# Two edge passes of a graph network: five PSUM banks, a fifteen-pair ring, and VectorE's steps at four distances

## The reference

```
q, k, v = linear maps of x, in 8 heads of 32                    # layer one
score   = clip(sum(q[dst] * k[src]) / sqrt(32), -10, 10)        # per edge and head
alpha   = exp(score - max) / sum over the edges of dst
wv      = segment_sum(alpha * v[src], dst)
x       = feat + (wv @ Wp.T + bp)
h       = layernorm(x) * ln_g + ln_b
out     = x + (gelu(h @ W1.T + b1) @ W2.T + b2)
x       = layernorm(x_in + out)

z       = leaky_relu(x @ W_s.T [src] + x @ W_t.T [dst])         # layer two
e       = z @ W_attn.T                                          # one number per edge
alpha   = exp(e - max) / sum over the edges of src
agg     = segment_sum(alpha * x[src], dst)
out     = layernorm(x + (agg @ W_fc.T + b_fc))
```

## Time and profile before

| | |
|---|---|
| median of three runs | 4053.36 us |
| the profiled execution, its own time | 4052.72 us |
| its span, first to last instruction | 4050.9 us |
| mean granted TensorE clock | 0.766 of 2.4 GHz |
| busy: PE / DVE / ACT / POOL | 2350.9 / 2223.8 / 1218.1 / 1941.0 us |
| HBM, mean | 172 GB/s |

### The profile page before, as it was taken

The page is one execution under the profiler, slowest core; times in us unless marked ns, Lnnn a source line. Parts: engine busy times, 40 slices in busy tenths (PEclk is TensorE's granted clock), DMA queues, the critical chain, the costliest instruction groups (busy, mean ns, idle before and its releaser), DMA issues. The chain is left out here.

```text
span 4050.9 us, 56408 instructions
## 1 busy us (share of the span) xinstructions
PE 2350.9 (58%) x11454; PEld 1705.1 (42%) x11455; DVE 2223.8 (55%) x6089; ACT 1218.1 (30%) x3239; POOL 1941.0 (48%) x1970
## 2 busy tenths in 40 slices
PE   4666666666666665887333333333333396777776
PEld 2344444444444444675122222222222195566555
DVE  5565565555555563334344444444444596677675
ACT  0255555555555553333122222222222200111111
POOL 0255555555555552212655656655555303444443
PEclk9888888888888887898565666666666656888998
DMA  4666665665666662113667677666766605666664
GB/s 140 196 175 176 176 177 174 180 181 169 177 178 179 176 182 84 65 63 100 207 205 205 206 210 209 200 202 203 205 200 200 181 0 164 200 205 198 193 208 148
DMA packets 365706, 698.61 MB, mean 172 GB/s; under 512 B 77317, under 2 KB 247039, under 8 KB 365674
## 3 DMA queue, kind: packets, MB, share of 16 engines
q0 software_dynamic: 134784, 425.63, 36.1%
q1 hardware_dynamic: 220602, 256.40, 20.2%
q10 hardware_dynamic: 10288, 16.23, 1.1%
HBM read 597.23 MB, written 100.85 MB: 172 GB/s over the span
## 5 line engine op out<-in xcount | busy, mean ns | idle before, releaser
L878 PE MATMUL ps_px<-sb_parts,sb_bits 128*128 x4860 | 886.7, 344 | 902.9 <-DVEq L1590 362.3
L759 POOL DMA_INDIRECT sb_ring<-kv_rows,sb_idx x810 | 792.3, 978 | 723.8 <-DVE sb_msg L1458 377.5
L878 PEld LDWEIGHTS ps_px<-sb_parts,sb_bits 128*128 128x128 bf16 x4860 | 566.5, 121 | 1238.4 <-DVEq L1590 586.7
L888 PE MATMUL ps_pa<-sb_msg,sb_onehot 128*128 128x264 f32 x1620 | 567.5, 483 | 433.1 <-DVE sb_msg L1458 349.0
L1125 ACT ACTIVATE sb_bits<-sb_bits 128x256 bf16<-128x256 bf16 x810 | 322.7, 409 | 1019.2 <-remote 725.9
L1443 DVE TENSOR_TENSOR sb_prod<-ps_px,sb_ring 128x512 f32<-128x512 f32 x405 | 278.7, 688 | 573.7 <-remote 339.9
L888 PEld LDWEIGHTS ps_pa<-sb_msg,sb_onehot 128*128 128x128 f32 x1620 | 345.0, 235 | 551.3 <-DVE sb_msg L1458 373.6
L759 POOL DMA_INDIRECT sb_ring<-proj_rows,sb_idx x324 | 311.7, 962 | 321.8 <-issue 156.1
L759 POOL DMA_INDIRECT sb_w<-narrow_rows,sb_idx x324 | 310.1, 957 | 207.4 <-DVEq L1590 113.0
L759 POOL DMA_INDIRECT sb_w<-feat_rows,sb_idx x162 | 158.6, 979 | 426.1 <-issue 190.3
L1593 DVE SCALAR_TENSOR_TENSOR sb_prod<-sb_msg,sb_attn_hi 128x256 f32<-128x256 f32 x810 | 300.5, 421 | 0.7 <-issue 0.7
(11 more groups left out here) (242 smaller groups left out, 3070.2 us busy)
## 6 DMA issues: line engine op xcount, KB each, us to landing
sb_bits<-dst_short SPq DMA_DIRECT2D x280, 192.0 KB
x_edges<-sb_ring SPq DMA_DIRECT2D x54, 768.0 KB
sb_slots<-x_edges SPq DMA_DIRECT2D x54, 768.0 KB
x_edges<-sb_slots SPq DMA_DIRECT2D x27, 768.0 KB
sb_w<-x_edges SPq DMA_DIRECT2D x27, 768.0 KB
sb_msg<-lo_rows SPq DMA_DIRECT2D x28, 576.0 KB
sb_ring<-kv_rows,sb_idx POOLq DMA_INDIRECT x810
kv_rows<-sb_slots ACTq DMA_DIRECT2D x25, 256.0 KB, 2.8
```

What stands on the lines that cost most here:

```text
L759: pool.indirect_dma_start(out=out[:, i, :], out_offset=None, in_=rows, in_offset=bass.IndirectOffsetOnAxis(ap=idx[:, 2 * p + i:2 * p + i + ...
L878: mm = pe.matmul(px[:, j, 0:width], onehot_t[:, j, :], flat(visit_parts[:, bass.ds(parity, 1), a, 0:width]), start=(a == 0), stop=(a == 2))
L888: mm = pe.matmul(pa[:, 0:C + H], onehot[:, j, :], msg[:, j, :], start=(p == 0 and i == 0), stop=True, skip_group_check=True)
```

## The change

In pass one:
- The ring of gathered keys and values grows from 5 to 15 pairs of slots, `kv_pairs`: six in `ring`, three in `slots`, six behind the node parts in `parts`. Each pair of a visit has its own slot and its own semaphore; the semaphores are shared with pass two.
- `px` holds a pair in one bank (two halves of 256 columns). Five banks serve five pairs (FLIGHT = 5), and the sixth takes the sums of the pairs from 8 on (EARLY), so that VectorE can copy `pa` at pair 10. Expansion is issued AHEAD = 9 pairs ahead of the sum.
- VectorE's order within pair p becomes: clip of p + 3, product of p + 6, scores of p + 4, message of p. The steps at a visit's end are spread over pairs 1 to 5 of the next visit.
- Messages go to `wide`, a ring of five pairs; scores have five places. Edge one-hots keep three.
- The node one-hots are made six tiles at a time, in place, in a room for all 30 tiles of a visit (`hots_t`), four groups ahead.
- SyncE stores a visit's projected rows two visits behind, at the end of its round, and the load of x (`load_inputs(0)`) goes behind the pass.

In pass two the node one-hots work the same way, `zbuf` has five pairs, the slot is freed by the row step itself, and the three small steps come once a visit over 30 tiles; two columns of each tile are kept for them by a copy (`low_dots`), one a pair.

The diff, cut to its core:

```diff
+FLIGHT = 5
+AHEAD = 9
...
-        kv_slots = ring_flat[:, 0:S * 2 * C].rearrange("p (j c) -> p j c", j=S)
+        kv_rooms = [ring_flat[:, 0:6 * 4 * C], slots[:, 0:3 * 4 * C], parts_f[:, kv_at:kv_at + 6 * 4 * C]]
+        kv_pairs = [room[:, i * 4 * C:(i + 1) * 4 * C].rearrange("p (j c) -> p j c", j=2) for room, n in zip(kv_rooms, (6, 3, 6)) for i in range(n)]
...
-                        gather_pair(0, p, kv_slots[:, two(p), :], kv_rows, gathered[0][p % SLOTS])
+                        gather_pair(0, p, kv_pairs[p], kv_rows, gathered[p])
...
-                pe.wait_ge(hot_t[L], v * PAIRS + p + 2)
+                if p % RING == 0:
+                    pe.wait_ge(hot_t[L], v * HALVES + p // RING + 2)
...
-                for j in flight(p):
+                for i in (0, 1):
+                    into = px[:, p % FLIGHT, i * C:i * C + width] if L == 0 else px[:, 2 * (p % RING) + i, 0:width]
                     for a in range(3):
-                        mm = pe.matmul(px[:, j, 0:width], onehot_t[:, j, :], flat(visit_parts[:, bass.ds(parity, 1), a, 0:width]),
+                        mm = pe.matmul(into, hots_t[L][:, 2 * p + i, :], flat(visit_parts[:, bass.ds(parity, 1), a, 0:width]),
                                        start=(a == 0), stop=(a == 2))
...
+                if p == EARLY and earlier is not None:
+                    pe.wait_ge(nd, earlier * ND + NDS["acc"])
+                into = pa if p < EARLY else px[:, FLIGHT]
...
+            def node_onehots(L, v, h):
+
+                act.wait_ge(far[L], v * HALVES + h + 2)
+                act.activation(hots_t[L][:, half(h), :], hots_t[L][:, half(h), :], ACT.Relu, bias=1.0, scale=-1.0).then_inc(hot_t[L], 1)
...
-                if p + 2 < end:
-                    products(*ahead[1])
-                if p + 1 < end:
-                    clipped(*ahead[0])
-                messages(v, p)
-                if p + 2 < end:
-                    scores(*ahead[1])
...
+                for p in range(PAIRS):
+                    if earlier is not None and 1 <= p <= len(FINISH):
+                        finish(earlier, FINISH[p - 1])
+                    if p + 3 < PAIRS or not last:
+                        clipped(*later(v, p + 3))
+                    if p + 6 < PAIRS or not last:
+                        products(*later(v, p + 6))
+                    if p + 4 < PAIRS or not last:
+                        scores(*later(v, p + 4))
+                    messages(v, p)
+                    if p == EARLY + 2:
+                        sums_kept(v)
...
-                        dve.wait_ge(zs, base + RING + R)
-
-                        dve.tensor_tensor(dots[:, 1], dots[:, 0], zbuf[:, :, C], ALU.add).then_inc(zs, 1)
...
+                        dve.wait_ge(slots_free[1], v * PAIRS + p + 1 + PAIRS)
+                        dve.tensor_copy(low_dots[:, :, 2 * p:2 * p + 2].rearrange("p c j -> p j c"), zbuf[:, pair(p), C:CW])
...
+                    dve.tensor_tensor(dots[:, 1], dots[:, 0], low_dots[:, 0], ALU.add).then_inc(zs, 1)
...
-            load_inputs(0)
             sp.wait_ge(y_clear, 16)
             first_pass()
+            load_inputs(0)
```

More of the change, by code:

```diff
@@ L270, in build @@
         q_ready = sem("q_ready")
-        gathered = [[sem(f"gathered{L}_{p}") for p in range(n)] for L, n in enumerate((SLOTS, PAIRS))]
+        gathered = [sem(f"gathered{p}") for p in range(PAIRS)]
         gathered_x = {p: sem(f"gathered_x{p}") for p in range(PAIRS) if not streamed(p)}
@@ L394, in places, with landed, pair, half @@
             return slice(2 * (p % RING), 2 * (p % RING) + 2)
-        def two(p):
-            return slice(2 * (p % SLOTS), 2 * (p % SLOTS) + 2)
+        def landed(eng, L, total, v, p):
+            eng.wait_ge(gathered[p], (v + total) * 32 + 32 if L else v * 32 + 32)
+        def pair(p):
+            return slice(2 * (p % FLIGHT), 2 * (p % FLIGHT) + 2)
+        def half(h):
+            return slice(h * R, (h + 1) * R)
+        def later(v, p):
+            return (v, p) if p < PAIRS else (v + 1, p - PAIRS)
         def chunk(p):
@@ L568, in visit @@
                             node_parts(node, parity)
-                        if L == 0 and h == 3 and earlier is not None:
-                            products_out(earlier)
                     fetched(v, range(PAIRS - SLOTS, PAIRS))
                     indices(after, THIRDS - 1)
+                    if L == 0 and earlier is not None:
+                        products_out(earlier)
                 def first_parts():
@@ L935, in _ @@
             parity, = value()
-            for p in range(4):
+            for p in range(AHEAD):
                 expand(0, C, parity, 0, p)
@@ L1142, in exps @@
                 act.wait_ge(summed, v * PAIRS + p + 1)
[L1143 removed]
+                act.activation(sums_in[:, pair(p), C:C + H], score[:, p % FLIGHT], ACT.Exp, scale=SCORE_SCALE).then_inc(exp1, 1)
             def window_nodes(v, earlier=None):
                 if earlier is not None:
[L1149 removed]
+                    act.wait_ge(far_e, (earlier + 1) * PAIRS)
                     act.sem_inc(act_seen, 1)
@@ L1181, in visits @@
-                    if p + 1 < PAIRS:
-                        edge_onehots(v, p + 1)
-                    if earlier is not None and p == 2:
+                            node_distances(0, at, h)
+                        if p % RING == 1:
+                            node_onehots(0, at, h)
+                    if p + 1 < PAIRS:
+                        edge_distances(t0, v, p + 1)
+                    elif not last:
+                        window_nodes(v + 1, v)
+                        edge_distances(t0, v + 1, 0)
@@ L1184, in visits @@
+                    if p:
+                        edge_onehots(v, p - 1)
+                    elif earlier is not None:
+                        edge_onehots(earlier, PAIRS - 1)
+                    if earlier is not None and p == 10:
                         sums_copied(earlier)
-                    if earlier is not None and p == 6:
+                    if earlier is not None and p == PAIRS - 1:
                         product_copied(earlier)
-                    if not last and p == PAIRS - 3:
-                        node_distances(0, v + 1, 0)
-                        node_onehots(0, v + 1, 0)
@@ new lines, in _, with visits @@
+            FINISH = ["acc", "den0", "den1", "den2", "agg"]
+            def visits(v, earlier=None, last=False):
+                for p in range(PAIRS):
[10 more added lines that the diff above has]
+                        sums_kept(v)
@@ L1507, in _ @@
+            for p in range(6):
+                if p >= 3:
+                    clipped(0, p - 3)
+                products(0, p)
+                if p >= 2:
+                    scores(0, p - 2)
+            visits(0)
+            with dve.Fori(0, total - 2) as u:
+                visits(dve.snap(u + 1), u)
+            visits(last_visit(dve), visit_before(dve), last=True)
+            for step in FINISH:
+                finish(last_visit(dve), step)
             dve.sem_inc(nv, 1)
@@ new lines, in _ @@
+                    rows(0)
+                    for p in range(PAIRS):
+                        if p + 1 < PAIRS:
+                            rows(p + 1)
+                        attend(p)
+                    dve.wait_ge(zs, v * len(ZS) + ZS["dots"])
+                    dve.tensor_tensor(dots[:, 1], dots[:, 0], low_dots[:, 0], ALU.add).then_inc(zs, 1)
+                    dve.wait_ge(zs, v * len(ZS) + ZS["low"])
+                    dve.tensor_tensor(dots[:, 2], dots[:, 1], low_dots[:, 1], ALU.mult).then_inc(zs, 1)
@@ L1616, in _ @@
+                    dve.wait_ge(zs, v * len(ZS) + ZS["masked"])
+                    some = e_all[:, bass.ds(t0, G)]
+                    dve.tensor_tensor(some, some, dots[:, 2], ALU.add).then_inc(zs, 1)
+                    dve.wait_ge(zs, v * len(ZS) + ZS["added"])
+                    dve.sem_inc(dve_seen, 1)
             for c in range(THIRDS):
```

253 lines of the change are left out of this document (111 added, 142 removed).

## The result

The changed kernel takes 4004.69 us (median of four runs, 3987.71 to 4020.03) against 4052.74 for the kernel before in the same runs: a ratio of 0.988, 95% interval 0.985 to 0.991, 48 us less. Forecast was 3925. Both later comparisons gave the same ratio (0.989 and 0.988). The profiled execution took 3997.64 us, its span is 3995.8.

The account below looks back on a forecast made before the run. It took gather runs over some 7 us, which nearly stop the other engines, as the limit. From 4052.7: -100 (ring), -35 (pass two), +6 (edges) = 3924, stated as 3925 us; range 3700 to 4110.

Parts of the forecast that it names:

- What bounds the kernel: Both edge passes: made of waits, no engine full; long gather runs nearly stop the other engines and limit this change.
- over some 7 us: Both edge passes: gather runs longer than this nearly stop other engines until 1 to 2.5 us after the run ends.
- The ring, -100 us: Pass one: 15 pairs of slots instead of five take it from 3.46 to 3.21 us a pair, -100 us.
- the stop of "3 us": Pass one, POOL: pause assumed after each 10.5 us gather run, making a cycle of 13.5 us for 4.2 pairs.
- Rival C: Pass one doesn't move, run and stop lengths change but not their sum; 4024, or up to 4053; chance 0.18.
- D: Pass one slower: POOL fills 15 slots in one run, starves the others, then waits for them; 4113; chance 0.18.
- Banks and distances: Pass one: five PSUM banks and VectorE's four distances remove 153.2 us of expansion waits; counted within the ring's sum.
- Visit's end: Pass one: steps spread over the next visit, one add more (12 us of VectorE), stalls go; left inside 2.15 us a pair.
- ScalarE's one-hots: Node one-hots for three pairs at a time, three activations become one; ScalarE has slack, so worth nothing and costing nothing.
- Pass two, -35: Pass two: VectorE's tail once a visit, less added copies, and slots told free earlier; -35 us, ends 0 and -90.
- The edges, +6: Pass one's edges: +4 us for x loaded ahead of the sums' load, +2 us for one-hots built at the start.
- Rule E: Pass two: 405 fp32 copies on VectorE lock GpSimd out and hold gathers up, +75 us; 4034; chance 0.05.

Follow-up runs that it names:

- half_count: Changed kernel, but in pass one only the first of a pair's two gathers is issued and its tile read twice; 3426.6 us, 0.845 of the kernel before.
- the third set: Later starved set of runs, with both kernels profiled again: changed kernel unedited 4008.0 us (ratio 0.989), kernel before 4059.6 us in one run.
- message_first: Changed kernel with VectorE's message step first of its four steps in a pair; 3270.3 us (0.978) in the set without starvation, 3987.1 us (0.984) repeated starved.
- spaced2: Changed kernel with every gather, plus a 128x160 fp32 addition on POOL after each pair's gathers in pass one; 3818.9 us, 0.958 of the kernel before.
- filler2: Changed kernel, pass one without each pair's second gather, a 128x420 fp32 addition on POOL after each remaining gather; 3880.7 us, 0.958 of the kernel before.

## Why the prediction was wrong

**What bounds the kernel** held: gathers without a pause nearly stop the other engines, and neither bytes nor slots set the pace. What I had called "over some 7 us" begins at 5 in the changed kernel.

**The ring, -100 us**, is the step that failed, and in it the stop of "3 us". The sum has 4.2 pairs in a run, so 96 stops, 289 us, beside the 1013 us of POOL's own gathers: that is the 1300 us forecast. The gathers without the stops took 1017 us, as put, and the runs came as forecast too: 4.0 pairs on average, 33 runs of four pairs and 37 of five among 101. But the 100 stops last 366 us, 3.7 on average, 4.3 at the median, and 4.7 to 4.9 in the cycle shown: 77 of the 83 us that pass one took over the forecast.

I took the stop from the earlier trace rows, where the ring is five deep, though the sum itself says that the release takes 1.5 us and the message then still has to be made: in the cycle shown VectorE starts 1.6 us behind the run, its message ends 4.1 us behind it, and POOL goes on 0.8 us later. With 4.7 in place of 3 and nothing else changed, the sum gives 5.2 pairs in 17.6 us, 3.41 us a pair; pass one took 3.42, against 3.45 before.

Two other numbers were off and nearly cancel: VectorE's full work ends at five microseconds and not at seven, and it needs 1.97 us a pair and not 2.15. The mechanism was the one I named and the form of the sum was right; one of its numbers, put 0.7 to 1.9 us too short, ate most of the term. No run has runs of this length with shorter stops, so this rests on the sum and on the measured stops. Rival C had the sentence that came nearest: the run and stop lengths change and their sum hardly does. That its 4024 is 19 us from the result is in part luck, since it takes 35 us for pass two, where 51 and 43 were measured.

I also argued against D that VectorE frees a slot each 2 us "once it goes, so that a full ring makes short runs". Over a third of the runs did become five pairs long, D's point, and the pass was no slower.

**Banks and distances**, counted within the ring: the wait for the expansion went from 153.2 us in 95 waits to 116.2 in 48, not to near zero. It too goes with the gathers: half_count shows VectorE at 1.97 us a pair with nothing late. My 2.15 was high: steps follow each other 1.87 to 1.89 us apart where nothing waits (half_count), not 2.04.

**Visit's end**: no cost shown in the floor of half_count, but a new place to stand: the add at L1492 waits 109 us for "remote" in 16 visits, idle time that in the kernel before fell to the product.

**ScalarE's one-hots**: free, as put. **Pass two, -35**: -51 was measured, and -43 in the third set, inside its ends of 0 and -90. How it divides among tail, one-hots and slots told earlier wasn't tried. That VectorE's slack makes the starved stretches harmless there was wrong: spacing gave 37 us more (1225 to 1188, in two sets whose kernels before are 8 us apart). The copies have a mean of 210 ns by the trace, above my upper end of 185, and didn't hurt.

**The edges, +6**, were put too small. From the last gather to POOL's first batch step are 33 us before and 50.8 after, 18 more (16 in the third set); the +4.1 at that step is what is left when the gathers end 13 us earlier. The parts were wrong too. The load of x is no cost on the path: from the store of the last sums to the issue of the sums' load are 5.85 us before and 6.33 after. The visit's end is longer by 2.6 us from the last message to that store. And the ring's drain was left out: the last message ends 7.7 us behind the last gather before (1557.2), 22.8 us after (1558.6), since POOL may be 15 pairs ahead and not five. That is 15 of the 18, and it gives back the 13 us by which the gathers end earlier. Counted to the last message, the five-pair ring's pass one and the new one's are as long (1557.2 and 1558.6).

**Rule E** on the locked port: beside the 405 copies the gathers of pass two take 962 to 977 ns on average, after 953 to 961 before. Even if the copies were the cause of all of it, that is some 11 us over 810 gathers and not 75, and pass two got shorter. E is out.

## What to carry to other kernels

Where one engine issues gathers back to back and "remote" waits of several engines end together after its runs, look first for space between the gathers: here a deeper ring only traded the length of a run against that of a stop. Look also whether the profile lost records in the same places. Before a stop is put into a sum, follow the slot's release through every step behind it, and count the ring's drain at the end of the pass. And test the condition as well as the kernel: the kernel before and message_first were both over 700 us faster in one set of runs, where the same cure cost time.

## What the runs showed of the hardware

- Gathers 1.25 us apart go with starvation of VectorE, ScalarE, TensorE and SyncE from about five microseconds on, in the result's runs and in four of the five sets of experiments, and in none of the kernels of the other. 0.50 us of other work on POOL after every second one nearly cures it. What carries the starvation, and why one set was free of it, stays open: no row names it. Bytes (0.62 or 0.37 DMA share), POOL's busy time (1015 of 1230 us in spaced2) and late rows (2.4 us at any place in a run) are excluded, and the chip's number was the same in a starved set and in the free one. The writing of the profile's records is not excluded: in the changed kernel's runs of gathers over half of the updates are missing, in the free set under 1 in 100.
- Where TensorE idles in between, its mean granted clock is lower: 0.80 in pass one of the changed kernel (busy 869 of 1387 us), 0.96 in message_first (780 of 1042) and 0.99 in half_count (729 of 792).
- A long addition on POOL holds VectorE up where a gather doesn't. The message step of filler2, and below it of half_count (busy us, mean ns):

```profile
L1483 DVE TENSOR_TENSOR sb_wide<-sb_parts,sb_wide 128x512 f32<-128x512 f32 x148 | 273.3, 1847 | 0.0
```

```profile
L1477 DVE TENSOR_TENSOR sb_wide<-sb_parts,sb_wide 128x512 f32<-128x512 f32 x156 | 105.8, 678 | 0.0
```

  The message reads two operands from SBUF; the product (one of them in PSUM) has a mean of 678 to 681 ns in both. The Trainium skill (SBUF — State Buffer, section "SBUF: two separate sides") says that a VectorE operation with two SBUF inputs and a GpSimd operation that reads SBUF lock each other out for a whole instruction. This case agrees that there is a lock, and not on its length: in filler2 the message is 1.17 us longer on average beside additions of 0.89 that don't get longer, and 1.97 us long where the addition starts inside it. Beside the additions of 0.50 us in spaced2 the messages have means of 689 to 704 ns. The same section of the Trainium skill says that DMA and compute can't slow one another and that TensorE and ScalarE never wait on anyone. By bytes that holds here; beside runs of gathers the trace has ScalarE idle up to 12.35 us, by a way that the page doesn't tell.
